# The product of the tile h with its inverse block scales moves from VectorE to GpSimd

## The reference, cut to what matters

```python
def fp4_quant_dequant(x):
    xb = x.reshape(shape[:-1] + (shape[-1] // BLOCK, BLOCK))      # BLOCK = 16
    scale = jnp.maximum(jnp.max(jnp.abs(xb), axis=-1, keepdims=True) / 6.0, 1e-12)
    xn = xb / scale
    idx = jnp.searchsorted(_MID, jnp.abs(xn))
    return (_GRID[idx] * jnp.sign(xn) * scale).reshape(shape)
...
gate = fp4_linear(x, w_gate)
y = fp4_linear(x, w_up)
h = jax.nn.silu(gate) * y
return fp4_linear(h, w_down)
```

## Time and profile before

| what | value |
|---|---|
| runs | 2240.13, 2242.16, 2244.68 us; median 2242.16 |
| span of the profiled execution | 2238.9 us |
| TensorE matmul busy | 2002.6 us (89%) |
| VectorE busy | 1754.4 us (78%) |
| ScalarE busy | 1149.2 us (51%) |
| GpSimd busy | 1108.9 us (50%) |
| h product on VectorE (L829, 128x704) | 128 of 881 ns, 112.7 us |
| DMA | mean 40 GB/s |

### The profile page before, as it was taken

The page is one execution under the profiler, slowest core; times in us unless marked ns, Lnnn a source line. Parts: engine busy times, 40 slices in busy tenths (PEclk is TensorE's granted clock), DMA queues, the critical chain, the costliest instruction groups (busy, mean ns, idle before and its releaser), DMA issues.

```text
span 2238.9 us, 37879 instructions
## 1 busy us (share of the span) xinstructions
PE 2002.6 (89%) x10532; PEld 1581.4 (71%) x10532; DVE 1754.4 (78%) x3548; ACT 1149.2 (51%) x2132; POOL 1108.9 (50%) x1643
## 2 busy tenths in 40 slices
PE   2787899899989999899999999899998999977776
PEld 1554677677777777678876777687776777766665
DVE  6234788788878888698877888698887888788876
ACT  2664555555644555455554565455554556433332
POOL 2222455466545555356544556455553555454543
PEclk9999999999999999999999999999999999999998
DMA  2111011111110111111111111111111111000000
GB/s 78 53 52 43 34 48 47 36 42 48 48 40 29 48 43 44 40 48 41 46 35 39 43 46 41 40 48 34 43 49 39 43 44 39 29 19 20 24 20 15
DMA packets 77087, 90.51 MB, mean 40 GB/s; under 512 B 8880, under 2 KB 59952, under 8 KB 76848
## 3 DMA queue, kind: packets, MB, share of 16 engines
q1 hardware_dynamic: 76848, 87.73, 11.9%
HBM read 37.37 MB, written 16.78 MB: 24 GB/s over the span
## 4 chain that ended last, share of the span: by engine, by line
PE 61%; issue 9%; DVE 6%; ACT 4%; POOL 4%; POOLq 0%; DVEq 0%; ACTq 0%
PE pgu L489 18%; PE pd L489 11%; PE pd L537 7%; PE pa L489 5%; PE pb L489 5%; PE pc L519 4%; PE pc L571 4%; PE pe_ L631 2%; PE pa L559 1%; PE pc L496 1%; POOL hbuf L432 1%; PE pe_ L548 1%; POOL rs L439 1%; DVE hbuf L989 1%; DVE hbuf L835 1%
## 5 line engine op out<-in xcount | busy, mean ns | idle before, releaser
L489 PE MATMUL pgu<-wgu_hi,xqT 128*128 128x512 f32 (+1 forms) x1536 | 426.3, 386 | 0.9 <-issue 0.9
L489 PE MATMUL pd<-wd_hi,hqT 128*128 128x256 f32 (+1 forms) x1536 | 334.4, 299 | 18.6 <-DVE r L1011 15.5
L489 PEld LDWEIGHTS pgu<-wgu_hi,xqT 128*128 128x128 f32 x1536 | 279.1, 189 | 75.7 <-issue 27.6
L537 PE MATMUL pd<-wout,g 128*128 128x256 f32 x1024 | 262.7, 401 | 55.6 <-DVE hqT L979 36.4
L489 PEld LDWEIGHTS pd<-wd_hi,hqT 128*128 128x128 f32 (+1 forms) x1536 | 255.9, 190 | 57.2 <-issue 23.8
L945 DVE SCALAR_TENSOR_TENSOR acc<-xps,cw,acc 128x512 f32<-128x512 f32 x256 | 248.5, 971 | 25.1 <-POOL acc L429 24.4
L418 POOL TENSOR_SCALAR rs<-mv 128x1 f32<-128x1 f32 x128 | 61.5, 480 | 396.7 <-DVE mv L1026 228.9
L537 PEld LDWEIGHTS pd<-wout,g 128*128 128x128 f32 x1024 | 191.0, 197 | 92.6 <-issue 69.4
L740 ACT ACTIVATE hqT<-pe_ 128x512 fp32r<-128x512 f32 x128 | 76.2, 595 | 331.6 <-PE pe_ L631 331.6
L402 POOL TENSOR_TENSOR xv<-xnq,qsx 128x256 f32<-128x256 bf16 x128 | 79.2, 619 | 322.8 <-DVE xnq L838 322.8
L489 PE MATMUL pgu<-wgu_lo,xqT 128*128 128x512 f32 (+1 forms) x768 | 228.1, 378 | 0.0
(11 more groups left out here) (133 smaller groups left out, 4670.0 us busy)
## 6 DMA issues: line engine op xcount, KB each, us to landing
xcr<-xcs SPq DMA_DIRECT2D x128, 256.0 KB, 2.3
xin<-in_L_attn_x_dram SPq DMA_DIRECT2D x32, 512.0 KB, 3.9
xres<-in_L_attn_x_dram SPq DMA_DIRECT2D x128, 128.0 KB, 2.1
out_dram<-outb SPq DMA_DIRECT2D x128, 128.0 KB, 1.7
szr<-in_L_attn_W_in_dram SPq DMA_DIRECT2D x1, 1024.0 KB, 7.4
szr<-in_L_ffn_w_down_dram SPq DMA_DIRECT2D x1, 704.0 KB, 8.6
szr<-in_L_ffn_w_gate_dram SPq DMA_DIRECT2D x1, 640.0 KB, 4.6
szr<-in_L_ffn_w_up_dram SPq DMA_DIRECT2D x1, 640.0 KB, 5.7
```

What stands on the lines that cost most here:

```text
L489: mm = pe.matmul(bank, lhsT, rhs, start=(m == 0), stop=(m == len(pairs) - 1))
L537: mm = pe.matmul(pd[:, 0:DM], g[:, (s + 1) % 2, c, j * P:(j + 1) * P], wout[:, c, :], start=(c == 0), stop=(c == NB - 1))
```

## The change

VectorE no longer multiplies the tile h. It multiplies only the 44 inverses of each row by -TIE, in place, and counts the link on. GpSimd then multiplies h by the spread inverses, in place in hbuf, and signals a new semaphore h_scaled, for which ScalarE's magnitude now waits. In GpSimd's queue the new product stands behind the dequantised x (and the copies of C) and ahead of the inverse square root of tile `to`. The quantisation of x keeps its product on VectorE.

```diff
+        h_scaled = sem("h_scaled")
...
+                    if exists(tg):
+
+                        pool.wait_ge(hq_link, 6 * tg + 4)
+                        pool.tensor_tensor(blocks(hbuf[:, FF:2 * FF]), blocks(hbuf[:, FF:2 * FF]),
+                                           spread(qsh[:, 2, :]), ALU.mult).then_inc(h_scaled, 1)
                     if exists(to):
 
                         wait_apart(pool, (mv1_done, to + 1), (r1_ready, to))
...
                     if exists(tg):
-                        act.wait_ge(hq_link, 6 * tg + 4)
+                        act.wait_ge(h_scaled, tg + 1)
                         act.activation(hbuf[:, 0:FF], hbuf[:, FF:2 * FF], ACT.Abs, scale=TWO22)\
                             .then_inc(hbig_ready, 1)
...
                     if exists(tg):
                         dve.wait_ge(hq_link, 6 * tg + 3)
-                        q_divide(h, small_h, h).then_inc(hq_link, 1)
+                        dve.tensor_scalar(small_h[2], small_h[2], -TIE, None, ALU.mult).then_inc(hq_link, 1)
```

## The result

The kernel before runs in 2243.4 us (median of four, 2240.1 to 2247.8), the changed one in 2266.3 us (median of four, 2263.5 to 2267.4). The ratio is 1.0101, with a 95% interval of 1.0082 to 1.0120: slower by 1.0%, 22.9 us. The profiled execution has a span of 2263.5 us, 24.6 more than before.

A forecast was written before the change was run, and what follows sets the result against it. TensorE's own work was taken to bound regular super-steps (60.09 of 61.00 us). Terms 12.6 - 4.2 + 4.3 + 0.7 = 13.4 us on a span of 2238.9 gave 2252.3, plus 3.3: 2255.6 us; range 2239 to 2272.

The forecast's parts named there:

- the forecast's own narrower range: Whole kernel: the forecast case, 2247 to 2265 us, with a chance of 0.55.
- much slower: Rival, chance 0.13, over 2265 us: GpSimd's product takes 1.77 us and L420 and L422 fall behind VectorE's rounding steps; 2286 us.
- The product's length: GpSimd's new 704-wide product of h takes 1.41 us, by the weight preparation's rows; bounds 0.88 and 1.77.
- The chain of h: From the scaled inverses' start to the first rounding step L835: 2.54 us instead of 1.86, so 0.68 later.
- The root behind the product: Inverse square root behind the product in GpSimd's queue: no loss, L420's median down from 1174 ns.
- Slot 2 to 3: L432 ends 0.53 us later; less 0.07 margin, TensorE's transposes of h stall 0.45 us, 28 times: 12.6 us.
- Slot 0 to 1: In 21 regular super-steps the stall is absorbed by existing waits and L422 comes 0.2 us earlier: -4.2 us.
- Slots counted as no stall: Slots 3 to 0 and 1 to 2: gap ahead of the transposes wider than a microsecond, so no stall.
- The boundary: Slot 0 at seven boundaries: softplus behind the later magnitude, TensorE's wait for dB 0.62 us longer each: 4.3 us.
- Tail: In the tail the transposes have 1.1 us to spare; only the last tile's bare chain adds 0.7 us, once.
- Hidden: Rival, chance 0.18: the stall from slot 2 to 3 is only 0.2 us, 3.5 us in all; 2242 to 2246 us.
- faster: Rival, chance 0.14: the product takes 0.73 us, so no stalls, and the shorter chain over L422 wins 5 us; 2237 us.

The follow-up runs named there:

- e2: The kernel before, with the magnitude also waiting for bn_aggr of r1 and nothing new on GpSimd: 2261.8 us, ratio 1.0086.
- e5: The changed kernel with the 44 inverses scaled ahead of the residual sum r1 on VectorE instead of behind it: 2230.6 us, ratio 0.9953.
- e12: The kernel before with bn_stats and bn_aggr of r1 ahead of the product on VectorE: 2264.1 us, ratio 1.0099.
- e1: The changed kernel without the new product on GpSimd, h left unscaled: 2221.9 us, ratio 0.9902.
- e6: The changed kernel with GpSimd's product over only 352 of 704 columns, half of h left unscaled: 2224.5 us, ratio 0.9914.
- e11: The changed kernel with VectorE's copy of the state projection ahead of the residual sum r2 in slot 1 of a boundary: 2259.2 us, ratio 1.0072.
- e3: The changed kernel with GpSimd's history copy and first tap ahead of the new product: 2305.6 us, ratio 1.0277.
- e4: The changed kernel with a boundary's softplus ahead of the magnitude in ScalarE's queue: 2288.7 us, ratio 1.0203.
- e8: The kernel before with ten unused matmuls on TensorE ahead of the partial state, at eight places: 2229.4 us, ratio 0.9948.
- e7: The changed kernel with ten unused matmuls on TensorE ahead of the partial state, at eight places: 2254.3 us, ratio 1.0052.

## Why the prediction was right, and where its size was off

The direction and the mechanism held, and the time, 2266.3 us, lies in the range, 10.7 above the forecast. It lies outside the forecast's own narrower range, though, which ended at 2265, and so where I had put *much slower* with a chance of 0.13; the mechanism of that rival didn't come. Measured against the kernel before, the loss was 22.9 us where I had summed 13.4. The sum is nearer than its terms deserve: one term was too large by 6 us, one that I had put at nothing was 5, and the two cancel by luck. The boundary alone was too small by 14. A small thing besides: I added 3.3 us as what lies around the span, but in every profiled execution on record the time is 1.8 or 1.9 us above the span, and the rest of the 3.3 was the spread between executions.

**The product's length.** 1.41 us predicted from the weight preparation's rows; 1.39 measured, 128 times. The rivals that rest on it (0.73 and 1.77) are out. So is the 1.53 us worked out from the rate in the Trainium skill, "GPSIMD Engine Reference", section "Elementwise — side-by-side cycle accounting": the trace is 0.14 us below it.

**The chain of h.** 2.54 us from the scaled inverses to the first rounding step predicted, 2.50 measured. e2 shows that this lateness alone carries 18.6 us of the 22.9, and e5, with the product as long but earlier, that without it nothing of the loss is left outside the tail.

**The root behind the product.** No loss there, and its median down from 1174 ns: 567 in all 128. Right. That VectorE's rounding steps and GpSimd's instructions exclude each other held too, but in one order I was wrong: I let the first tap stand against L838. It is the three-element copy in front of it that stands there (0.18 us, now 0.90), and the tap follows when it is let go.

**Slot 2 to 3.** L438 ends 7.31 us from r1, where L432 ended 6.88: 0.43 later, predicted 0.53. The margin was a little larger than my 0.07, and of TensorE's lateness the distance keeps 0.24 us, not 0.45. By 28 that is 6.7 us and not 12.6. This term was too large by 6, and it is the first step that was mis-sized. The waits of L637 for L438 came 52 times with 0.6 us in the mean, where I had asked for 28 and more at 0.3 to 0.6.

**Slot 0 to 1.** -0.2 predicted, -0.27 measured, by 21 is 5.7 us won. The mechanism was the one I named, L422 earlier; e12 and e5 show when it is let go.

**Slots counted as no stall.** 1→2 is right (17.61, 17.63). 3→0 is not: 0.23 us longer, in e2 0.28, and not at all in e1, e5 and e6. The transposes of h come on time there (8.30 us from r1, 8.29 before), as I said. It is the state projection, which stands further behind. From the timeline of the changed kernel, and then of the one before:

```profile
1316.66 0.62 ACT L765 ACTIVATE xcs<-acc 128x512 f32<-128x512 f32 x1
...
1316.90 0.63 PE L495 MATMUL pb<-xt_hi,win_lo 128*128 128x512 f32 x2
...
1317.49 0.97 PEld L577 LDWEIGHTS pc<-wxp,xcs 128*128 128x128 f32 x8 [0.40 <-issue]
...
1317.52 1.05 PE L577 MATMUL pc<-wxp,xcs 128*128 128x33 f32 x8
```

```profile
1304.73 0.63 PE L489 MATMUL pb<-xt_hi,win_lo 128*128 128x512 f32 x2
...
1305.19 0.97 PE L571 MATMUL pc<-wxp,xcs 128*128 128x33 f32 x8
```

ScalarE started on the projection's input xcs 0.55 us before the last z product (1304.18 in the kernel before) and now does so 0.24 before it; the projection follows 0.62 behind instead of 0.46, and its first weight load shows a wait of 0.40. I read this as VectorE's lateness passed on over the quantisation of x and ScalarE; the profile names no releaser there, so it is argued, while that it goes with the late magnitude is shown. I had looked at one chain to TensorE in that slot, and there are two. It costs 21 x 0.23 = 4.8 us. Between the first boundary and the last there are 24 regular distances 2→3 and 18 of each other kind, and they come to 5.8 - 4.9 + 4.1 + 0.4 = 5.4, against the 5.5 measured there.

**The boundary is the term that was mis-sized.** Predicted: 0.62 us for dB in each of seven, 4.3 us. Measured: 18.6. The wait for dB is what I predicted, 3.05 us where it was 2.41: 0.64. With seven it makes 4.5. At the last of the seven the wait grows less, so their sum grows by 4.4 (17.4 to 21.8). Two things stand beside it that I had at nothing.

The first is the y product's wait of 0.78 us for ssm L931, which wasn't there before: 4.7 us in six places. I hadn't followed the lateness past dB to what VectorE does next in the boundary's own order.

The second is TensorE's clock. The seven stretches that the last column of the table adds up hold the same number of matmuls in both kernels. Their sums, before and after (length; busy PE, PEld, DVE, ACT, POOL):

```profile
sum 413.97, PE 349.44 PEld 262.38 DVE 287.59 ACT 188.19 POOL 170.91; mean PE 49.92 PEld 37.48 DVE 41.08 ACT 26.88 POOL 24.42
```

```profile
sum 432.65, PE 357.24 PEld 270.59 DVE 269.68 ACT 189.83 POOL 204.18; mean PE 51.03 PEld 38.66 DVE 38.53 ACT 27.12 POOL 29.17
```

TensorE is busy for 7.8 us longer with the same work. By the traces' clock records the lower of the two levels, 1.2 GHz instead of 2.4, was granted for 61 us of these stretches before and for 82 after. Half of the time that TensorE was busy in it is my estimate of what it cost. With the two waits it gives this account, in us more than in the kernel before, over the seven boundaries:

| kernel | longer by | wait for dB | wait for ssm | clock (estimate) | left |
|---|---|---|---|---|---|
| after | 18.6 | 4.4 | 4.7 | 8.7 | 0.8 |
| e1 no product | -1.0 | -0.1 | 0.0 | -1.9 | 1.0 |
| e2 late magnitude | 11.7 | 3.8 | 3.8 | 3.2 | 0.9 |
| e5 scale first | -0.7 | 0.0 | 0.0 | -1.0 | 0.3 |
| e11 projection first | 11.9 | 4.2 | 1.5 | 6.0 | 0.2 |
| e12 stats first | 12.3 | 4.8 | 4.3 | 1.6 | 1.6 |

So it closes to 1.6 us in each of these (in e3, e4 and e6, worked out in the same way, to 1.4), and it says too what e2 leaves out: 5.5 of its 6.9 us are clock.

The filling doesn't speak against this. It lowers the estimated cost of the clock at the boundaries from 29.1 to 14.3 us in the kernel before (e8) and from 37.9 to 23.3 in the changed one (e7), by nearly the same, and so leaves the distance between the two. And e7 and e8 differ by 13.9 us at the boundaries, not by 24.9; much of the other part goes with the clock too, as e7 has 60 us at the lower level outside the boundaries and e8 has 37.

Where the additional low clock of the changed kernel comes from is shown in part. At three of the seven boundaries a stretch of it starts about a microsecond behind the end of the new wait for ssm; in e11, where most of that wait is gone, there is none in that place. How much of the clock's part belongs to the change, and how much to where its idle times happen to fall, is open: the kernels with the same late magnitude (after, e2, e12) range from 1.6 to 8.7 us. It isn't the chance of one execution, at least: the four of the changed kernel have a mean granted clock of 0.970 to 0.973, the five of e2 0.973 or 0.974.

**Tail.** Predicted nothing but 0.7 for the last tile; 0 up to the last r1 and 1.3 behind it.

**The rivals.** *Much slower* didn't come by its mechanism, since the product takes 1.39 us and the inverse square root is never held. *Hidden* and *faster* didn't come either, but *faster* had a true core: the relief of VectorE is worth 17 to 21 us (e1, e6), four times the 5 that I gave it, since with an early magnitude slot 0→1 wins 0.9 us and not 0.24. The change pays for this with a product that ends 0.65 us too late, and e5 has the relief without the lateness by moving one short instruction.

## What to carry to other kernels

When work moves to another engine, ask first when its input is ready and start it there: here the change cost 23 us with the product behind r1 and won 11 with it ahead of r1, and 0.65 us decided. In a pipeline over several engines follow a late result through every queue that it passes, two or three instructions beyond the first wait, and do so apart for each irregular stage, as 21 of the 127 distances, those around the seven boundaries, held three quarters of the loss. And when the waits don't add up to the loss, look at TensorE's granted clock over the same stretch: a short wait can cost more than its length. Before putting a long GpSimd instruction into a gap, look at which VectorE instruction comes next, however small.

## What the hardware showed that I hadn't expected

A VectorE product of 128 x 44 elements took 1.19 us instead of 0.17 while GpSimd's 512-wide sum ran (e3), and a GpSimd copy of three elements a row took 0.90 instead of 0.18 beside VectorE's rounding step. In these pairs the second waits for the whole of the first, however small it is itself. The Trainium skill, "SBUF — State Buffer", section "Who interferes with whom", says that the two engines can contend for the port and that the first to issue keeps it for its whole instruction; both rows agree. That the second one's wait is recorded as its own duration, and not as idle time, is how these rows show it. The held VectorE product in e3 reads one tile only, so it isn't only VectorE's two-input instructions that are held; beside the new product the one-input L1024 was not (0.43 us, as alone).

GpSimd's float32 product with inverses spread over blocks of 16 took 1390 ns for 704 elements and 0.79 us for 352, so 1.7 ns an element, while the sum of two full tiles took 1.28 to 1.29 us for 512.

Ten matmuls of no use, in a wait of 2.4 to 3.1 us at eight places, made the whole kernel 12 us faster, twice (e7, e8). The matmuls behind the wait took 3.63 us instead of 5.33 at most of them, with the mean granted clock of the kernel before at 0.977 and that of e8 at 0.985.
